# A new slot layout for the projections of an attention step, with the weighted sums of the values two at a time

## The reference: what is computed

```python
x = norm(x + scan_mix(x))             # u = x B^T; h_t = A h_(t-1) + u_t; h W^T + b
x = norm(x + attention(x, ctx))       # 16 heads of 16, rotary q and k, band |i-j| <= 50, output Wo
x = norm(x + experts(x))              # router: silu(x W1) W2, softmax over tokens, top 64 of each
                                      # of 16 experts, gated FFN of width 512, added back to its rows
```

## Time and profile before

| | |
|---|---|
| time, median of 3 runs | 1072.51 us (1072.12 to 1072.58) |
| the profiled execution: its time, its span | 1072.09 us, 1070.3 us |
| busy over the span | PE 991.9 (93%), PEld 845.4 (79%), DVE 729.6 (68%), ACT 591.3 (55%), POOL 672.7 (63%) |
| stretch 54 to 405 (steps of attention) | PE busy 23.67 to 26.15 of every 27 us |
| PE's wait for `x2cur`, stretch 80 to 405 | 9.7 us in 11 times |
| OX of two neighbouring steps | starts at 213.14 and at 239.25 us |

### The profile page before, as it was taken

The page is one execution under the profiler, slowest core; times in us unless marked ns, Lnnn a source line. Parts: engine busy times, 40 slices in busy tenths (PEclk is TensorE's granted clock), DMA queues, the critical chain, the costliest instruction groups (busy, mean ns, idle before and its releaser), DMA issues.

```text
span 1070.3 us, 21269 instructions
## 1 busy us (share of the span) xinstructions
PE 991.9 (93%) x6436; PEld 845.4 (79%) x6436; DVE 729.6 (68%) x2168; ACT 591.3 (55%) x1234; POOL 672.7 (63%) x784
## 2 busy tenths in 40 slices
PE   4799999999989998879999999999999999999990
PEld 3578778777877877658898888888888888888880
DVE  4678888888877798757554787565556756765633
ACT  1155565556565555456656555555555556555642
POOL 5556666666666565267757665776666767666543
PEclk8899999999999999899999999999999999999995
DMA  6344344433333332525676666666676666666636
GB/s 191 84 103 98 100 106 103 103 99 102 102 101 97 85 81 70 182 94 168 156 223 124 160 141 168 136 158 152 160 218 158 141 155 149 147 155 143 184 54 176
DMA packets 114918, 142.56 MB, mean 133 GB/s; under 512 B 15104, under 2 KB 88064, under 8 KB 114688
## 3 DMA queue, kind: packets, MB, share of 16 engines
q1 hardware_dynamic: 86432, 105.56, 34.2%
q0 software_dynamic: 24576, 33.57, 18.1%
q10 hardware_dynamic: 3808, 2.22, 0.7%
HBM read 90.70 MB, written 29.36 MB: 112 GB/s over the span
## 4 chain that ended last, share of the span: by engine, by line
PE 52%; ACT 1%; DMA 1%; POOL 1%; issue 1%; DVE 0%; ACTq 0%; POOLq 0%; SPq 0%
PE gate_bank L1349 16%; PE attn L1349 16%; PE value_bank L1349 16%; PE turn_bank L1359 2%; DMA last<-acc_rows 0%; ACT last L1590 0%; DMA acc_rows<-y,slots_now 0%; PE attn L1432 0%; PE attn L1406 0%; POOL acc_rows L1294 0%; DVE stats L1627 0%; DVE hidden L1620 0%; ACTq L1594 0%; ACT w_hi L1482 0%; POOL rstd L167 0%
## 5 line engine op out<-in xcount | busy, mean ns | idle before, releaser
L1294 POOL DMA_INDIRECT acc_rows<-y,slots_now x128 | 205.6, 1607 | 137.4 <-issue 73.4
L787 ACT ACTIVATE probsT<-scoreT 128x356 f32<-128x356 f32 x256 | 117.7, 468 | 137.6 <-PE scoreT L618 113.3
L945 DVE CUSTOM_DVE_ANT_0 scored<-score,band 128x178 f32<-128x178 f32 x512 | 149.9, 337 | 63.3 <-PE score L589 59.4
L1620 DVE TENSOR_TENSOR hidden<-gate,value_bank 128x512 f32<-128x512 f32 x128 | 87.9, 687 | 152.7 <-ACT gate L1495 152.6
L1495 ACT ACTIVATE gate<-gate_bank 128x512 f32<-128x512 f32 x128 | 76.6, 598 | 188.3 <-PE value_bank L1349 188.3
L1349 PE MATMUL attn<-w_hi,h_hi 128*128 128x256 f32 x512 | 146.1, 285 | 0.2
L1349 PE MATMUL attn<-w_hi,h_lo 128*128 128x256 f32 x512 | 143.3, 280 | 0.0
L1349 PE MATMUL attn<-w_lo,h_hi 128*128 128x256 f32 x512 | 143.3, 280 | 0.0
L589 PE MATMUL score<-k_stack,q_stack 96*128 96x178 f32 x512 | 123.8, 325 | 7.2 <-DVE nmax L945 4.2
L589 PEld LDWEIGHTS score<-k_stack,q_stack 96*128 96x128 f32 x512 | 88.9, 194 | 37.1 <-DVE nmax L945 17.3
L618 PE MATMUL scoreT<-q_stack,k_stack 97*128 97x356 f32 x256 | 116.5, 456 | 0.0
(11 more groups left out here) (214 smaller groups left out, 2374.9 us busy)
## 6 DMA issues: line engine op xcount, KB each, us to landing
arena<-in_w SPq DMA_DIRECT2D x96, 512.0 KB, 4.0
k_stack<-high_k SPq DMA_DIRECT2D x128, 64.0 KB, 2.2
q_stack<-high_q SPq DMA_DIRECT2D x128, 64.0 KB, 2.3
arena<-in_xT SPq DMA_DIRECT2D x16, 256.0 KB, 2.9
arena<-in_x SPq DMA_DIRECT2D x16, 256.0 KB, 3.1
arena<-in_cT SPq DMA_DIRECT2D x16, 256.0 KB, 3.7
k_stack<-low_k SPq DMA_DIRECT2D x64, 64.0 KB, 2.3
q_stack<-low_q SPq DMA_DIRECT2D x64, 64.0 KB, 2.2
```

Source lines behind the costliest of these rows:

```text
L787: nc.scalar.activation(probsT[g % 2][:, u % HG, :, :].rearrange("p a s -> p (a s)"), scoreT[u % 2][:, 0:2 * SPAN], ACT.Exp, scale=1.0 / DH ...
L945: op = nc.vector.tensor_tensor_reduce(scored[t % 2][:, q, :], score[t % 2][:, q * SPAN:(q + 1) * SPAN], band[:, q, :], -1.0, BIG, ALU.add, ...
L1294: nc.gpsimd.indirect_dma_start(dram["acc"][c], bass.IndirectOffsetOnAxis(ap=now[:, m:m + 1], axis=0), y[m][:], None, compute_op=ALU.add).t ...
L1620: nc.vector.tensor_tensor(hidden[f % 2][:], gate[f % 2][:], value_bank[f % 2][:], ALU.mult).then_inc(hidden_ready, 1)
```

## The change

It moves work between slots and adds none.

- `ORDER`: OX goes from the first bank to the second, between O and V. So V waits for OX to be read, and OX for O.
- PE: K from slot 1 to 0, right behind X; both halves of O in slot 2, back to back; OX from 13 to 9; R from 15 to 13. Q, U, Y and V stay in 3, 5, 8 and 11.
- The gathers, four in a step, go from slots 2, 6, 10, 14 to two in slot 1 and two in slot 9 (`GATHERED`).
- ACT: K read in slot 1 and its high part in 3 (before 2 and 5); `keep_values` in 2 and 10 (before 7 and 15); `x2T` in 10, R read in 14.
- DVE: rotation of K in 2, statistics of O in 3, odd additions in 4 and 10, `x2cur` in 7.
- POOL: the low part of K right behind its rotation, and the second norm's `inverse_deviation` ahead of the rotation of Q.
- The router: silu in slot 2 of step 10 (before 9), logits in slot 15 of step 10 (before step 11, slot 13), and the eight rounds of the top 64 in slots 4 and 10 of steps 11 to 15 (before slots 1, 4, 7 and 14 of steps 12 to 15).

```diff
-        ORDER = (("X", "Q", "U", "Y", "OX"), ("K", "O", "V", "R"))
+        ORDER = (("X", "Q", "U", "Y"), ("K", "O", "OX", "V", "R"))
...
-        NORMAL = {"O": (4, 7), "statistics": 8, "estimate": 9, "normalise": 11, "OX": 13, "x2T": 14, "R": 15, "r1": 15}
+        NORMAL = {"O": (2, 2), "statistics": 3, "estimate": 4, "normalise": 7, "OX": 9, "x2T": 10, "R": 13, "r1": 14}
...
+        GATHERED = {1: (-4, -3), 9: (-2, -1)}
...
                     if not hoisted(it):
                         cosine(it, 0)
                         rotate(it, 0)
+                        lower(it, 0)
                     cosine(it, 1)
+                if there(it, "O"):
+                    inverse_deviation(it, "O")
                 if there(it, "Q"):
                     rotate(it, 1)
-                    if not hoisted(it):
-                        lower(it, 0)
                     lower(it, 1)
...
-                    if t in (2, 6, 10, 14):
-                        gather(it, t)
-                    if t == 1 and there(it, "K") and not hoisted(it):
-                        keys(it)
+                    if t in (1, 9):
+                        for g in GATHERED[t]:
+                            gather(it, g)
...
+                    if t == 0 and there(it, "K") and not hoisted(it):
+                        if it.fixed and it.i == 11:
+                            pe.wait_ge(logits_kept, 1)
+                        keys(it)
...
-                    if t == 2 and there(it, "K") and not hoisted(it):
-                        biased(it, 0)
...
+                    if t == 1 and there(it, "K") and not hoisted(it):
+                        biased(it, 0)
-                    if t in (7, 15):
+                    if t in (2, 10):
                         keep_values(it, t)
...
-                    if t in (3, 11) and has(it, group(t, 15)) and not only(it, NB, t, 11):
-
-                        p = group(t, 15) // 2
+                    if t in (odd_at(it), 10) and has(it, -1) and not only(it, NB, t, 10):
+
+                        p = -1 if t == 10 else -2
...
-                    if t == 3 and there(it, "K") and not hoisted(it):
+                    if t == 2 and there(it, "K") and not hoisted(it):
                         rotated(it, 0)
...
-                    for n, (i, at) in enumerate(((12, 7), (12, 14), (13, 1), (13, 14), (14, 1), (14, 14), (15, 1), (15, 4))):
+                    for n, (i, at) in enumerate(((11, 10), (12, 4), (12, 10), (13, 4), (13, 10), (14, 4), (14, 10), (15, 4))):
```

More of the change, by code:

```diff
@@ L322, in slot, with odd_at @@
             return DRAIN if it.fixed and it.i >= NB else NORMAL
+        def odd_at(it):
+            return 3 if it.fixed and it.i >= NB else 4
         def only(it, i, t, at):
@@ L685, in step @@
                         project(it, "Q", wq, x1T)
[L686 to L695 removed]
+                    for n in range(TT):
+                        if t == slot(it)["O"][n] and there(it, "O"):
+                            if n == 0:
+                                begin(it, "O")
+                                pe.wait_ge(attnT_ready, it.lin(NPAIR, -NPAIR))
+                            for g in range(NPAIR):
+                                mm = nc.tensor.matmul(bank("O")[:, n * D:(n + 1) * D], attnT[it.r % 2][:, g, n * P:(n + 1) * P],
+                                                      wo[:, g, :], start=(g == 0), stop=(g == NPAIR - 1))
+                            if n == TT - 1:
+                                mm.then_inc(ready["O"], 1)
                     if t == 5 and there(it, "U"):
@@ L706, in step @@
                         transposed(it, "OX", x2cur)
[L707 to L715 removed]
+                    if only(it, NB - 1, t, 11):
                         pe.wait_ge(route.picked, 1)
@@ L742, in step @@
                         mm.then_inc(ready["R"], 1)
+                    if only(it, 10, t, 15):
+                        pe.wait_ge(rw2_set, 1)
+                        pe.wait_ge(silu_done, 1)
+                        pe.wait_ge(freed["R"], uses(it, "R") + FREED_EARLY["R"])
+                        for c in range(GB):
+                            mm = nc.tensor.matmul(bank("R")[:, 0:S], rw2_placed[:, c, :], r1[:, c * S:(c + 1) * S],
+                                                  start=(c == 0), stop=(c == GB - 1))
+                        mm.then_inc(logits_ready, 1)
             for i in (-2, -1):
@@ L876, in step @@
                         biased(it, 1)
-                    if t == 5 and there(it, "K") and not hoisted(it):
+                    if t == 3 and there(it, "K") and not hoisted(it):
                         heighten(it, 0)
@@ L884, in step @@
                         heighten(it, 1)
[L885 removed]
+                    if only(it, 10, t, 2):
                         act.wait_ge(freed["R"], GB + FREED_EARLY["R"])
```

37 lines of the change are left out of this document (5 added, 32 removed).

## The result

The changed kernel takes 1145.12 us (median of 4 runs, 1142.45 to 1149.24) against 1072.55 of the kernel before: ratio 1.068, interval 1.064 to 1.072, 72.6 us slower. I had forecast slower, 1118 with a range up to 1142, so the direction held, the new waits came nearly as walked, and the size came out too small, 3 us over the top of the range. The profiled execution is the slowest of the four (1149.24 us, span 1147.4), 77.1 us over the span of before.

The account below looks back on a forecast made before the run. PE bounds the kernel; its step becomes 24.5 own work, 4.05 waits and 0.7 restarts, 29.3 against 26.1. 14 steps at 3.2 more give 45, so 1072.5 + 45 = 1118 us, range 1094 to 1142.

Parts of the forecast that it names:

- PE bound, one wait at OX: Kernel before: PE is busy 93% of the span and idles once a step, 0.86 at OX for `x2cur`.
- What is taken away, 1.6: Per step: 1.0 at OX, 0.4 from paired gathers, 0.2 from K and OX placement, leaving PE's own work at 24.5.
- its term of 1.0: Wait at OX for `x2cur`, 0.86, and about 0.15 to get going again, gone from each step.
- The restart of 0.15: PE's loss in getting going after a wait, taken as the middle of 0 to 0.3; five new ones make 0.7.
- V 1.4: V, due at 19.62 in a step, waits 1.4 for OX to be read by ACT (`x2T`, 21.0).
- U 0.8: U, due at 8.86 in a step, waits 0.8 for ACT to read Q (`raw_q`, 9.66).
- O 0.5: O, due at 3.03 in a step, waits 0.5 for ACT to read K (`raw_k`, 3.54).
- R 0.65: R, due at 24.06 in a step, waits 0.65 for V to be read by DVE (24.7).
- Y 0.5: Y, wanted at 13.5 in a step, waits 0.5 for DVE's scan, done at 14.0.
- Score 8 0.2: Score of slot 8, wanted at 12.7 in a step, waits 0.2 for DVE's maxima of slot 6, done at 12.8.
- I set these against each other.: Outside the steady step: losses in steps 0 and 1 and from the router's moves, gains in the last, counted as cancelling.
- The clock: Rival: short idle times lower PE's clock in every loop step, 56 us more, 1174, or half of it, 1146; chance 0.07.

Follow-up runs that it names:

- b_x2_first: The kernel before with `x2cur` put ahead of the odd addition in VectorE's slot 11; 1087.12 us, ratio 1.016.
- b_odd_late2: The kernel before with `x2cur` first and slot 11's odd addition in slot 14, ACT's reciprocal in 15; from step 10 back in 11 and 12; 1066.98 us, ratio 0.9961.
- a_high5: The changed kernel with ACT's high part of K back in slot 5; 1159.28 us in one run.
- a_unrolled: The changed kernel with TensorE's loop over the steps 2 to 9 written out; 1137.81 us, ratio 1.063.
- a_shift: The changed kernel with 17 semaphore increments that compute nothing ahead of TensorE's first step; 1138.65 us, ratio 1.062.
- b_shift: The kernel before with 239 semaphore increments ahead of TensorE's first step, to put its loop where the changed kernel's lies modulo 256 instructions; 1102.79 us, ratio 1.029.
- a_q_first: The changed kernel with ACT's read of Q (`raw_q`) ahead of the exponential of slot 4 instead of behind it; 1153.05 us, ratio 1.078.

## Why the prediction fell short

- *PE bound, one wait at OX.* Right as a reading of PE, too short as a reading of the kernel. (The 23.67 ahead of the prediction is a stretch behind 405; up to 405 the lowest is 23.97. Nothing rests on it.) `b_x2_first` shows that the wait at OX was VectorE's queue: with `x2cur` first, score 14 waited 1.16. Both engines were full from the scan to the values; VectorE's 4 idle us of 26 lay elsewhere.
- *What is taken away, 1.6.* The wait at OX went, but its term of 1.0 was too large: without any wait the old layout's step takes 25.4 (`b_odd_late2`), so it was worth 0.65 to 0.7. With 0.7 instead of 1.0 PE's own work comes out at 24.8, and 24.8, 4.19 of waits and seven restarts of 0.15 make 30.0 where 29.9 was measured. The restart of 0.15 no run isolates.
- *The waits.* V 1.4: measured 1.23. U 0.8: 0.76. O 0.5: 0.54. R 0.65: 0.69. Y 0.5: 0.48. Score 8 0.2: 0.21. Sum 4.05 against 3.91, and one that I had not placed, score 0, 0.28. Each is right within 0.2, the step within 0.6 (29.3 against 29.9): 0.3 is the term of OX, 0.14 the waits, and the rest two more restarts than the sum had. The 0.6 in 14 steps is 8. Two causes were named wrongly: Y's wait is not VectorE's run, and U's wait has VectorE's close behind it.
- *The step that failed: "I set these against each other."* The prediction put all that lies outside the steady step at nothing, and the steps up to Q of step 2 cost 12.6, not 0. About 2 of it is only that O now stands ahead of Q. From Q of step 1 to Q of step 2, 7.3 of the 12.6, PE's waits come to 5.0 instead of 1.7, and PEclk is 0.95 instead of 1.00. The longest is U's, 1.85 for `raw_q` instead of 0.76, since ACT waits in slot 3 for GpSimd's `raw_k`; `a_high5` shows that cause, and also that without it a score waits instead. I had walked ACT's reads without the high part of K, which the change moved from slot 5 to 3.
- *The loop's end*, 8 of the 77, was no term of the prediction, and no row of before warned of it: the step there took 26.68, and 26.63 with the loop written out. `a_unrolled` and `a_shift` show its 7 us.
- *The clock.* I gave this rival a chance of 0.07, as a loss in every loop step. That did not come: in the loop, but for its end, PEclk is 1.00 at 4 us of idle time in seven pieces. It came in the late steps (stretches, columns as above; the pair of before, 409 to 436 and 436 to 460, has 0.94 in 27 and 0.86 in 24 us):

```profile
475.00:508.00 33.00, 26.57 (x209) 20.47 (x207) 20.75 (x101) 15.61 (x41) 14.95 (x20) 0.90 0.30 74
508.00:540.00 32.00, 25.16 (x161) 19.03 (x160) 19.59 (x92) 15.06 (x38) 11.06 (x18) 0.79 0.32 121
```

The missing share is 0.10 x 33 + 0.21 x 32 = 10.0 us, against 0.06 x 27 + 0.14 x 24 = 5.0. By the Trainium skill ("TensorE: Matmul & The Clock Gate", A second HAM failure mode: psum-queue depth-cycling) short idle times between groups make the clock go back and forth; the late steps agree, the loop's steps do not. No run here changed the clock alone, so these 5 us are read from rows and not shown by an experiment. They are also not all of it: over the whole span the mean granted clock is 0.962 against 0.975, a missing share of 43.6 us against 26.8. The 17 more are an upper bound of what the clock took, since PE is idle in part of them; about 4 lie ahead of Q of step 2 (0.88 in 103.6 us, 0.91 in 91.0), 3 to 4 at the loop's end, 4 between Q of step 10 and Q of step 14 (0.97, before 1.00) and 7 from there to the experts (0.83 in 81.5 us, 0.91 in 73.4). The late steps also have a wait that the sum of a step has not: score 8 waits 1.11 instead of 0.21 in the steps 12 and 13, where a round of the top 64 stands in slot 4.

In sum, by place: 77.1 = 45 forecast + 8 (0.6 a step; 5 of it in the loop) + 8 (loop's end) + 12.6 (first steps) + some 3 to 4 in the late ones. The steady step and the loop's end are shown by experiments, the first and the late steps only by rows. Why `b_shift` left the loop in memory stays open, and so does how much of the first steps' loss is the clock's (0.94 from 54 to 108) and how much is waiting.

## What to carry to other kernels

Ask of each product how long its bank's reader takes, counted from its end, and what stands between it and the next user of that bank; a step of back-to-back products is short on paper and waits at every bank. When one wait is taken away, look at what its releaser does next: three times here (`a_q_first`, `b_x2_first`, step 1 of `a_high5`) most of it or more came back at a score. Walk the first and last steps as well as the steady one, and read the step across a loop's jump for itself after every change of the code ahead of the loop.

## What the runs showed of the hardware that I had not expected

- A loop of TensorE held its code through a second pass or loaded it again (45 or 54 fetches of 16 KB), by 17 instructions ahead of it. The second case cost 8.8 in that step (5.9 idle, and PEclk 0.91 over 40 us) and 7 in the total.
- A semaphore increment on TensorE's queue took 0.13 to 0.16 us: with 239 of them ahead of it U starts at 37.69 us, 32.2 later than in the kernel before.
- One stretch at 1.2 GHz cost 1.7 us in a step that is otherwise alike (31.5 against 29.8, `a_q_first`). That kernel's loop waits 1.08 to 1.10 and 1.24 at its longest and has three such stretches away from its end; the changed kernel's, with 0.76 and 1.23, has none. What it takes for the clock to fall, these rows do not tell.
- `x2cur` took 1.68 in slot 7, where a low part of POOL runs from 172.17 to 173.53, and 0.73 in slot 11 of the kernel before, where POOL has only products of two columns. No run told the cause apart. The timeline of DVE, after:

```profile
172.00 1.68 DVE L971 TENSOR_SCALAR x2cur<-pre_O,mv_O,rstd_O 128x256 f32<-128x256 f32 x2
```

and before:

```profile
238.47 0.73 DVE L969 TENSOR_SCALAR x2cur<-pre_O,mv_O,rstd_O 128x256 f32<-128x256 f32 x2
```
